# First batch's feed-forward first layer as three products of rounded parts, in a two-layer AdaLN kernel

## The chip, the cores and the metric

The kernel runs on one NeuronCore of one Trainium2 chip. The metric is the device time of one execution in microseconds (us). TensorE (PE in the profile, its weight loads PEld) does the matrix products, VectorE (DVE) and ScalarE (ACT) the elementwise work, GpSimd (POOL) some of it, SyncE (SP) issues the transfers.

## The reference, cut to what matters

The program is two transformer-like layers. The change lies in the soft mixture of experts of the first one. For each of B = 2 batches it takes S = 2048 rows x of width C = 256, normed and modulated, and e x t = 8 x 128 slots:

```
logits = jnp.einsum('bsd,etd->bset', xn, se)
dispatch = jax.nn.softmax(logits, axis=1)
slots = jnp.einsum('bsd,bset->betd', xn, dispatch)
h = jax.nn.gelu(slots @ w1, approximate=False)      # w1: 256 x 1024
processed = h @ w2                                  # w2: 1024 x 256
combine = jax.nn.softmax(logits.reshape(b, s, e * t), axis=-1)
out = jnp.einsum('bnd,bsn->bsd', processed.reshape(b, e * t, d), combine)
```

`slots @ w1` is the feed-forward's first layer; only that of batch 0 is touched. All data is float32.

## The kernel before, in words

There is no scheduler. Each engine has a program written out by hand, in order, and semaphores join them. The function `soft_mixture` does this stage, batch after batch (b = 0, 1), and within a batch in three parts.

First, eight turns, one for each expert (`et` = 0 to 7). In a turn TensorE makes the logits of the next expert (`logits`, four banks of 512 columns in `pL`), ScalarE copies them to `raw[et]` (`keep`), VectorE takes their maxima (`maxima`) and ScalarE the exponentials (`exps`, tile `work`). TensorE turns the exponentials of the current expert in four groups (`transposes`), ScalarE copies the first two turned groups and VectorE the last two (`copy_t`, tile shown as `mod`), and TensorE multiplies them with xn (`slots`). VectorE divides by the sum (`scale_slots`); TensorE turns the result, and VectorE copies it into `slotsT` (`d_sp`; experts 0 to 3 in `d_sp0`, 4 to 7 in `d_sp1`). VectorE also keeps a running maximum over experts in `top` (`tops`).

Second, the feed-forward: `hidden(b, a, j)` is slots times w1 for half a of the slots (512 columns) and piece j of 8 of the hidden width, into one of four banks of `pL`; ScalarE applies the gelu from there (`gelu`); `outputs(b, et)` is the second layer. Between them `top` is turned, reduced and spread (`turn_tops`, `row_tops`, `spread_tops`), VectorE subtracts it from the logits (`shift`) and scales the outputs (`processed`), and ScalarE takes the exponentials (`weights`). Third, `combine` multiplies these with the processed slots, 16 tiles of rows.

The logits are made by `exact_matmul`: each float32 operand is split into a rounded part (type FR, fp32r, made by ScalarE: `turned_high`) and what is left of it (made by VectorE: `turned_low`, xTl = xT - xTh), and three products replace one:

```
    nc.tensor.matmul(out, ah, bh, start=start, stop=False)
    nc.tensor.matmul(out, al, bh, start=False, stop=False)
    return nc.tensor.matmul(out, ah, bl, start=False, stop=stop)
```

`hidden` before uses one plain float32 product in place of these. Such a product shows as two records in the trace. The turned rows lie in `xTh` and `xTl`. Once the last logits of a batch are read (`l_ready`), SyncE loads `w1` and `w2` over `xTl` (`feed_forward`), and `xTh` lies unused until the next batch's rows are turned.

## Time and profile before

| | |
|---|---|
| median of 3 executions | 1737.71 us (1735.82 to 1738.24) |
| the profiled execution's own time | 1735.53 us |
| its span in the trace | 1733.8 us |
| mean granted TensorE clock | 0.985 |
| PE busy, DVE busy, ACT busy, POOL busy | 94%, 70%, 42%, 31% |
| soft mixture, batch 0: eight turns | about 389 to 511 us of the span |
| its feed-forward | about 511 to 573 us |
| its combine, with the next batch's rows turned | about 573 to 632 us |

Times in the views are microseconds from the span's start. An idle time in square brackets is that of the engine before the instruction, with what ended it.

### The profile page before, as it was taken

Reading aid. Unit: us, or ns where it says so; the run is one execution under the profiler, and the core shown is the slowest. Engines: PE = TensorE matmul, PEld = TensorE weight load, DVE = VectorE, ACT = ScalarE, POOL = GpSimd, SP = SyncE. Lnnn points to the kernel's source line nnn. Section 1 sums busy time; section 2 is a strip of 40 time slices with the busy share of each in tenths; the row PEclk is TensorE's granted clock in tenths of the full one; section 3 lists DMA queues with packets and bytes.
Section 4 is the critical chain, followed back from the end, with each engine's and each line's share of the span. In section 5 each row is a group of like instructions: output and inputs, shape, how many; then the busy total and the mean of one; then the engine's idle time right before and its main releaser. Section 6 shows DMA issues by size and latency. Waiting matters only on the chain. (4 is left out here: it accounts for less than half of the span.)

```text
span 1733.8 us, 25488 instructions
## 1 busy us (share of the span) xinstructions
PE 1637.8 (94%) x9248; PEld 1378.4 (80%) x9248; DVE 1208.5 (70%) x2665; ACT 732.7 (42%) x1443; POOL 541.5 (31%) x443
## 2 busy tenths in 40 slices
PE   6999989989999999999988999999989999999996
PEld 4688878888876888867876888888768788989895
DVE  5777677764544556656797899999967945666663
ACT  3333333434323434435436666666521324454442
POOL 2100020000000002332344666566400023777764
PEclk9999999999999999999999999999989999999998
DMA  6000000010010000031115222222241124666553
GB/s 225 4 1 1 1 1 1 1 43 7 0 49 0 1 13 13 19 107 55 33 50 203 65 76 76 78 82 83 62 153 55 49 64 142 154 146 162 136 123 37
DMA packets 80248, 111.55 MB, mean 64 GB/s; under 512 B 15982, under 2 KB 60154, under 8 KB 79868
## 3 DMA queue, kind: packets, MB, share of 16 engines
q1 hardware_dynamic: 66172, 91.43, 16.5%
q0 software_dynamic: 12288, 17.31, 5.6%
q8 instruction: 75, 1.23, 0.3%
q10 hardware_dynamic: 1664, 1.18, 0.2%
q14 instruction: 49, 0.40, 0.1%
HBM read 81.59 MB, written 27.68 MB: 63 GB/s over the span
## 5 line engine op out<-in xcount | busy, mean ns | idle before, releaser
L2994 POOL DMA_INDIRECT out<-k_eo,idx x64 | 117.2, 1832 | 75.5 <-DVE k_eo L3086 60.8
L1883 POOL DMA_INDIRECT k_xe<-rows_dram,idx x64 | 82.4, 1288 | 179.5 <-DVE idx L2927 141.2
L1716 PE MATMUL d_pO<-d_sp,d_raw 128*128 128x257 f32 x512 | 116.1, 384 | 1.9 <-DVE x L1197 1.7
L1716 PEld LDWEIGHTS d_pO<-d_sp,d_raw 128*128 128x128 f32 x512 | 96.9, 192 | 16.6 <-DVE x L1197 2.4
L537 ACT ACTIVATE b_p<-b_pS,b_nmax 128x2048 f32<-128x2048 f32 (+14 forms) x32 | 40.6, 1270 | 139.8 <-DVE b_nmax L678 139.8
L61 PE MATMUL b_pO<-b_vh,b_ph 128*128 128x256 f32 x302 | 87.9, 291 | 4.4 <-DVE b_pl L660 4.3
L62 PE MATMUL b_pO<-b_vh,b_pl 128*128 128x256 f32 x302 | 85.6, 283 | 0.0
L63 PE MATMUL b_pO<-b_vl,b_ph 128*128 128x256 f32 x302 | 85.6, 283 | 0.0
L333 POOL TENSOR_TENSOR x<-x,b_vrow 128x256 f32<-128x256 f32 x32 | 24.0, 780 | 186.4 <-DVE b_hs L606 186.3
L2076 ACT ACTIVATE g_dlm<-d_cumb,mod 128x128 f32<-128x128 f32 x256 | 78.5, 395 | 3.6 <-DMA d_cumb<-cum_dram 3.6
L3045 ACT ACTIVATE k_act_g<-k_pg 128x512 f32<-128x512 f32 x64 | 38.3, 598 | 88.6 <-PE k_pu L63 88.6
L3099 DVE TENSOR_TENSOR k_hid<-k_act_g,k_pu 128x512 f32<-128x512 f32 x64 | 44.0, 688 | 44.2 <-ACT k_act_g L3045 43.6
L61 PE MATMUL k_po<-k_wh,k_hh 128*128 128x256 f32 x256 | 72.4, 283 | 2.1 <-issue 2.1
L1482 ACT COPY d_raw<-pL 128x512 f32<-128x512 f32 x64 | 37.4, 588 | 86.5 <-PE pL L63 86.5
L63 PE MATMUL k_po<-k_wl,k_hh 128*128 128x256 f32 x256 | 72.5, 283 | 0.0
L62 PE MATMUL k_po<-k_wh,k_hl 128*128 128x256 f32 x256 | 72.4, 283 | 0.0
L669 DVE TENSOR_REDUCE b_part<-b_pS 128x1 f32<-128x512 f32 (+3 forms) x86 | 53.1, 624 | 27.2 <-PE b_pS L63 26.8
L61 PE MATMUL b_pS<-b_kh,b_qh 128*128 128x512 f32 (+3 forms) x172 | 69.3, 403 | 1.4 <-DVE b_vl L652 1.4
L61 PE MATMUL pL<-d_winh,g_uh 128*128 128x128 f32 (+1 forms) x186 | 68.4, 368 | 0.2 <-DVE d_cs L2305 0.2
L660 DVE TENSOR_TENSOR b_pl<-b_pT,b_ph 128x512 fp32r<-128x512 f32 (+3 forms) x86 | 50.4, 619 | 25.0 <-ACT b_ph L529 25.0
L63 PE MATMUL pL<-d_winl,g_uh 128*128 128x128 f32 (+1 forms) x186 | 66.8, 359 | 0.0
L62 PE MATMUL pL<-d_winh,g_ul 128*128 128x128 f32 (+1 forms) x186 | 66.5, 358 | 0.0
(555 smaller groups left out, 5270.3 us busy)
## 6 DMA issues: line engine op xcount, KB each, us to landing
d_cumb<-cum_dram SPq DMA_DIRECT2D x32, 512.0 KB, 4.2
k_wf<-in_WgT SPq DMA_DIRECT2D x16, 512.0 KB, 3.9
k_wf<-in_WuT SPq DMA_DIRECT2D x16, 512.0 KB, 4.9
k_wf<-in_WdT SPq DMA_DIRECT2D x16, 512.0 KB, 6.8
rows_dram<-h_hx SPq DMA_DIRECT2D x32, 136.0 KB, 3.8
x<-in_x SPq DMA_DIRECT2D x8, 512.0 KB, 10.5
d_w<-in_w SPq DMA_DIRECT2D x4, 1024.0 KB, 6.2
uT_dram<-d_ug SPq DMA_DIRECT2D x16, 256.0 KB, 2.4
```

Of the source, the lines that this page charges most:

```text
L61: nc.tensor.matmul(out, ah, bh, start=start, stop=False)
L62: nc.tensor.matmul(out, al, bh, start=False, stop=False)
L63: return nc.tensor.matmul(out, ah, bl, start=False, stop=stop)
L537: nc.scalar.activation(pr[:, n % 2, 0:w], pS[:, bank[n]:bank[n] + w], ACT.Exp, bias=nmax[:, n % 2:n % 2 + 1], scale=scale, accum_out=esum[ ...
L660: nc.vector.tensor_tensor(pl[:, r, 0:w], src[:, 0:w], ph[:, r, 0:w].bitcast(F32), ALU.subtract).then_inc(s["lo_done"], 1)
L669: nc.vector.reduce_max(part[:, n % 2, g:g + 1], pS[:, bank[n] + g * GW:bank[n] + g * GW + width(n, g)], axis=AX).then_inc(s["part_done"], 1)
L1716: last = nc.tensor.matmul(pO[:, t % 2, 0:PW], raw[e][:, t * P:(t + 1) * P], proc[e], start=e == 0, stop=e == E - 1)
L1883: nc.gpsimd.indirect_dma_start(out=m.xe[:, e % 2, t, :], out_offset=None, in_=m.rows, in_offset=bass.IndirectOffsetOnAxis(ap=column(m, e, ...
L2076: nc.scalar.activation(le[:, b, h, :], cumb[:, b, h, :], ACT.Relu, bias=cs[:, b, 3, h:h + 1], scale=-1.0).then_inc(s["dd_done"], 1)
L2994: nc.gpsimd.indirect_dma_start(out=out, out_offset=bass.IndirectOffsetOnAxis(ap=column(m, e, t), axis=0), in_=eo[:, e % 2, t, :], in_offse ...
L3045: nc.scalar.activation(act_g[:, f % 2], pg[:, f % 2], ACT.Gelu).then_inc(s["gelu_done"], 1)
L3099: nc.vector.tensor_tensor(hid[:, f % 2], act_g[:, f % 2], pu[:, f % 2], ALU.mult).then_inc(s["hid_done"], 1)
```

## The change: what it does

- `hidden` of batch 0 uses `exact_matmul` on rounded parts and remainders of w1 and of the slots: 3 fp32r products for each float32 product (96 in place of 32). Batch 1 is as before.
- ScalarE rounds w1 (`first_weights_high`, two instructions) and the first half of the slots (`slots_high_of(0)`) after its last copy of turn 7, and the second half (`slots_high_of(1)`) after the third gelu. They are put where `xTh` lay.
- VectorE makes the remainders in place, over w1 and over the slots: `first_weights_low(0)` and `(1)` behind each of its two copies in turn 7, `slots_low(0)` behind these, `slots_low(1)` between the two `row_tops`.
- In batch 0 `tops(et)` moves from the end of turn et to its start (from the middle of turn 7 for et = 7).
- The semaphores `xT_high` and `xT_low` count the new parts too (SPLIT = 4), and each piece of `hidden` waits for `xT_low`.

```diff
+        sp0_at = nc.sbuf_base - ES * PW * 4
...
+        w1l = placed("w1l", [P, CH, HID], xTl_at, FR)
+        slots_lows = [placed(f"slots_low{a}", [P, CH, 512], at, FR) for a, at in enumerate((sp0_at, area + 136 * KB))]
+        w1h = placed("w1h", [P, CH, HID], area + 44 * KB, FR)
+        slots_high = [placed(f"slots_high{a}", [P, CH, 512], area + (52 + 4 * a) * KB, FR) for a in range(SH)]
...
+            def first_weights_low(k):
+                dve.wait_ge(s["xT_high"], NG + k + 1)
+                nc.vector.tensor_tensor(w1l[:, k], w1[:, k], w1h[:, k].bitcast(F32), ALU.subtract).then_inc(s["xT_low"], 1)
+
+            def slots_low(a):
+                dve.wait_ge(s["xT_high"], NG + CH + a + 1)
+                nc.vector.tensor_tensor(slots_lows[a][:], slotsT[a], slots_high[a][:].bitcast(F32), ALU.subtract).then_inc(s["xT_low"], 1)
...
                 for et in range(E):
+                    if not b and et:
+                        tops(b, et)
                     if b and 2 <= et < E - 1:
                         step_sizes(0, et - 2)
...
                     for g in range(2, NG):
                         copy_t(b, ("exp", et, g))
-                    if et == E - 1:
+                        if not b and et == E - 1:
+                            first_weights_low(g - 2)
+                    if not b and et == E - 1:
+                        slots_low(0)
+                    if b and et == E - 1:
                         tops(b, et)
                     scale_slots(b, et)
...
-                    elif et:
+                    elif b and et:
                         tops(b, et)
...
                 row_tops(b, 0)
+                if not b:
+                    slots_low(1)
                 row_tops(b, 1)
...
+            def first_weights_high(k):
+                act.wait_ge(s["w_in"], 32)
+                act.wait_ge(s["l_ready"], bank(0, E - 1, NG - 1))
+                nc.scalar.copy(w1h[:, k], w1[:, k]).then_inc(s["xT_high"], 1)
+
+            def slots_high_of(a):
+                await_copy(act, at[0, "slots", (a + 1) * ES - 1, 0])
+                nc.scalar.copy(slots_high[a][:], slotsT[a]).then_inc(s["xT_high"], 1)
...
+                    elif not b:
+                        for k in range(CH):
+                            first_weights_high(k)
+                        slots_high_of(0)
...
                 for j in range(HT):
                     gelu(b, 0, j)
+                    if not b and j == 2:
+                        slots_high_of(1)
...
+                dst, of = pL[:, j % 4 * 512:(j % 4 + 1) * 512], slice(j * P, (j + 1) * P)
+                if not b:
+                    pe.wait_ge(s["xT_low"], NG + CH + a + 1)
                 for k in range(CH):
-                    last = nc.tensor.matmul(pL[:, j % 4 * 512:(j % 4 + 1) * 512], w1[:, k, j * P:(j + 1) * P],
-                                            slotsT[a][:, k, :], start=k == 0, stop=k == CH - 1)
+                    if b:
+                        last = nc.tensor.matmul(dst, w1[:, k, of], slotsT[a][:, k, :], start=k == 0, stop=k == CH - 1)
+                    else:
+                        last = exact_matmul(nc, dst, w1h[:, k, of], w1l[:, k, of], slots_high[a][:, k, :],
+                                            slots_lows[a][:, k, :], k == 0, k == CH - 1)
```

What stands in a row on an engine is shown at three places. The first is TensorE's, at the start of batch 0's feed-forward, behind the turning of `top`; before:

```order
L1697 MATMUL d_pT<-ident,d_top_4961 128x128 x7
L1677 MATMUL pL<-d_sp0,d_w1_4964 128x512 [waits d_w_in,d_raw_done]
L1677 MATMUL pL<-d_sp0,d_w1_4964 128x512 x7
L1704 MATMUL d_pT<-ident,d_rmax 128x128 [waits d_rmax_done]
L1704 MATMUL d_pT<-ident,d_rmax 128x128 x7
```

The same place in the changed kernel, its first pieces:

```order
L1740 MATMUL d_pT<-ident,d_top_4961 128x128 x7
L61 MATMUL pL<-d_slots_high0_4970,d_w1h_4969 128x512 [waits d_xT_low,d_w_in,d_raw_done]
L62 MATMUL pL<-d_slots_high0_4970,d_w1l_4966 128x512
L63 MATMUL pL<-d_slots_low0_4967,d_w1h_4969 128x512
L61 MATMUL pL<-d_slots_high0_4970,d_w1h_4969 128x512
L62 MATMUL pL<-d_slots_high0_4970,d_w1l_4966 128x512
L63 MATMUL pL<-d_slots_low0_4967,d_w1h_4969 128x512
L61 MATMUL pL<-d_slots_high0_4970,d_w1h_4969 128x512 [waits d_xT_low]
```

Each piece j (two products before) has become six, and the first of each waits for the remainders as well.

The second place is VectorE's turn 7 of batch 0, from the copy that ends turn 6 on; before:

```order
L1163 COPY d_sp1_4974<-d_pT 128x2x128 [waits d_t_ready]
L1154 TENSOR_TENSOR d_top_4961<-d_top_4961,d_raw6_4971 128x2048 [waits d_top_done,d_raw_done]
L1161 COPY mod<-d_pT 128x512 [waits d_t_ready] x2
L1154 TENSOR_TENSOR d_top_4961<-d_top_4961,d_raw7_4972 128x2048 [waits d_top_done,d_raw_done]
L1170 RECIPROCAL d_rsum<-d_esum 128x1 [waits d_exp_done]
L1175 TENSOR_SCALAR mod<-d_pO,d_rsum 128x256 [waits d_t_ready,d_sl_ready,d_rsum_done]
L1163 COPY d_sp1_4974<-d_pT 128x2x128 [waits d_t_ready] x2
L1180 TENSOR_REDUCE d_rmax<-d_pT 128x8 [waits d_mt_ready] x2
```

The same place in the changed kernel:

```order
L1177 COPY d_sp1_4980<-d_pT 128x2x128 [waits d_t_ready]
L1168 TENSOR_TENSOR d_top_4961<-d_top_4961,d_raw7_4978 128x2048 [waits d_top_done,d_raw_done]
L1175 COPY mod<-d_pT 128x512 [waits d_t_ready]
L1126 TENSOR_TENSOR d_w1l_4966<-d_w1_4964,d_w1h_4969 128x1024 [waits d_xT_high]
L1175 COPY mod<-d_pT 128x512 [waits d_t_ready]
L1126 TENSOR_TENSOR d_w1l_4966<-d_w1_4964,d_w1h_4969 128x1024 [waits d_xT_high]
L1130 TENSOR_TENSOR d_slots_low0_4967<-d_sp0,d_slots_high0_4970 128x1024 [waits d_xT_high]
L1184 RECIPROCAL d_rsum<-d_esum 128x1 [waits d_exp_done]
L1189 TENSOR_SCALAR mod<-d_pO,d_rsum 128x256 [waits d_t_ready,d_sl_ready,d_rsum_done]
L1177 COPY d_sp1_4980<-d_pT 128x2x128 [waits d_t_ready] x2
L1194 TENSOR_REDUCE d_rmax<-d_pT 128x8 [waits d_mt_ready]
L1130 TENSOR_TENSOR d_slots_low1_4968<-d_sp1_4980,d_slots_high1_4971 128x1024 [waits d_xT_high]
```

One maximum has left the place between the copies and the reciprocal (the one ahead of the copies is now that of expert 7), and three subtractions have come in, one of them between the two copies.

The third place is ScalarE's, from the last two copies of turn 7 on; before:

```order
L1487 COPY mod<-d_pT 128x512 [waits d_t_ready] x2
L1493 ACT_TABLE_LOAD
L1493 ACTIVATE d_work_4973<-pL 128x512 [waits d_h_ready] x5
L1497 COPY d_top_4961<-d_pT 128x1024 [waits d_mb_ready]
L1493 ACTIVATE d_work_4973<-pL 128x512 [waits d_h_ready] x3
```

The same place in the changed kernel:

```order
L1518 COPY mod<-d_pT 128x512 [waits d_t_ready] x2
L1496 CAST d_w1h_4969<-d_w1_4964 128x1024 [waits d_l_ready,d_w_in] x2
L1500 CAST d_slots_high0_4970<-d_sp0 128x1024 [waits d_t_copied_d]
L1524 ACT_TABLE_LOAD
L1524 ACTIVATE d_work_4979<-pL 128x512 [waits d_h_ready] x3
L1500 CAST d_slots_high1_4971<-d_sp1_4980 128x1024 [waits d_t_copied_d]
L1524 ACTIVATE d_work_4979<-pL 128x512 [waits d_h_ready] x2
```

Three roundings stand ahead of the table load, and one among the gelus.

## Rows read from the trace of the kernel before

**Rows 1.** The page's busy times of TensorE and of its weight loads.

```profile
PE 1637.8 (94%) x9248; PEld 1378.4 (80%) x9248; DVE 1208.5 (70%) x2665; ACT 732.7 (42%) x1443; POOL 541.5 (31%) x443
```

**Rows 2.** TensorE's waits from 559.6 us to the end, the longest two.

```profile
PE pL L2424 <- ACT mod L2055: 4.8, 1, 4.8
PE i_pg L61 <- PEq L50: 3.0, 1, 3.0
```

**Rows 3.** TensorE's groups by form, 384 to 900 us: busy us, mean ns.

```profile
L1677 PE MATMUL pL<-d_sp,d_w 128*128 128x512 f32 x128 | 56.1, 593 | 0.0
L61 PE MATMUL pL<-d_xTh,o_seh 128*128 128x512 f32 x128 | 51.4, 402 | 0.0
```

**Rows 4.** TensorE by stretches: two of logits, then two of `hidden`.

```profile
439.29:444.87 5.58, 5.58 (x24) 1.00 0.00 0
632.53:643.55 11.02, 11.02 (x51) 1.00 0.00 0
511.50:518.37 6.87, 6.87 (x16) 1.00 0.00 0
544.98:558.90 13.92, 13.89 (x32) 1.00 0.00 0
```

**Rows 5.** Timeline of turn 7: start us, duration us.

```profile
500.97 0.59 ACT L1487 COPY mod<-d_pT 128x512 f32<-128x512 f32 x1 [0.64 <-PE d_pT L1657]
501.57 1.28 ACT L1493 ACT_TABLE_LOAD   x1
503.13 0.69 DVE L1161 COPY mod<-d_pT 128x512 f32<-128x512 f32 x1 [0.72 <-PE d_pT L1657]
505.10 3.62 PE L1667 MATMUL d_pO<-o_keys,mod 128*128 128x256 f32 x16
505.30 0.69 DVE L1161 COPY mod<-d_pT 128x512 f32<-128x512 f32 x1 [1.47 <-PE d_pT L1657]
505.91 2.28 DVE L1154 TENSOR_TENSOR d_top<-d_top,d_raw 128x2048 f32<-128x2048 f32 x1
508.11 0.15 DVE L1170 RECIPROCAL d_rsum<-d_esum 128x1 f32<-128x1 f32 x1
509.07 0.48 DVE L1175 TENSOR_SCALAR mod<-d_pO,d_rsum 128x256 f32<-128x256 f32 x1 [0.81 <-PE d_pT L1661]
513.42 0.60 ACT L1493 ACTIVATE d_work<-pL 128x512 f32<-128x512 f32 x1 [10.57 <-PE pL L1677]
```

**Rows 6.** Groups by form of roundings and subtractions elsewhere in this stage.

```profile
L1539 ACT CAST d_wogh<-d_wog 128x1024 fp32r<-128x1024 f32 x2 | 2.0, 1035 | 0.0
L1277 DVE TENSOR_TENSOR d_wogl<-d_wog,d_wogh 128x1024 fp32r<-128x1024 f32 x2 | 2.4, 1224 | 0.0
```

**Rows 7.** All engines by stretches while w1 and w2 arrive; DMA share, GB/s last.

```profile
489.90:495.00 5.10, 4.81 (x29) 4.06 (x28) 1.69 (x4) 3.62 (x5) 0.00 (x0) 1.00 0.77 261
495.00:497.50 2.50, 2.50 (x15) 2.27 (x14) 0.76 (x2) 0.00 (x0) 0.00 (x0) 1.00 0.90 307
497.50:499.00 1.50, 1.50 (x10) 1.27 (x9) 0.00 (x0) 0.00 (x0) 0.00 (x0) 1.00 0.00 0
```

**Rows 8.** Timeline of VectorE in turn 1, and one row of turn 2.

```profile
409.82 0.48 DVE L1175 TENSOR_SCALAR mod<-d_pO,d_rsum 128x256 f32<-128x256 f32 x1 [2.77 <-PE d_pO L1667]
411.74 0.69 DVE L1142 TENSOR_REDUCE d_part<-d_raw 128x1 f32<-128x512 f32 x1 [1.44 <-ACT d_raw L1482]
...
427.67 1.27 DVE L1142 TENSOR_REDUCE d_part<-d_raw 128x1 f32<-128x512 f32 x2
```

**Rows 9.** Timeline from the last shifts to the first combine.

```profile
546.39 8.89 DVE L1185 TENSOR_TENSOR d_raw<-d_raw,d_top 128x2048 f32<-128x2048 f32 x4
559.56 14.08 PE L1685 MATMUL d_pO<-d_w,d_work 128*128 128x256 f32 x64 [0.69 <-ACT d_work L1493]
560.82 14.51 ACT L1501 ACTIVATE d_raw<-d_raw 128x2048 f32<-128x2048 f32 x8
573.48 14.07 PE L1716 MATMUL d_pO<-d_sp,d_raw 128*128 128x257 f32 x64
```

**Rows 10.** All engines by stretches at the start of the last stage; granted clock behind POOL.

```profile
1435.00:1437.00 2.00, 0.00 (x0) 0.00 (x0) 1.22 (x1) 0.00 (x0) 0.00 (x0) 1.00 0.00 0
1437.00:1439.00 2.00, 1.78 (x5) 1.48 (x6) 0.00 (x0) 0.00 (x0) 0.96 (x2) 0.68 1.08 269
1439.00:1441.00 2.00, 2.00 (x6) 1.55 (x5) 0.00 (x0) 0.00 (x0) 1.70 (x2) 0.50 0.88 278
```

More of the change, by code:

```diff
@@ L905, in soft_mixture @@
         NH = NTB // 2
+        SPLIT = CH + SH
         upper_half = pL[:, HALF:T].rearrange("p (k n) -> p k n", k=CH)
@@ L1132, in turned_low @@
                 cols = slice(g * GW, (g + 1) * GW)
-                dve.wait_ge(s["xT_high"], n)
+                dve.wait_ge(s["xT_high"], n + (SPLIT if b else 0))
                 if b:
@@ L1630, in turn @@
                     if g >= 2:
-                        pe.wait_ge(s["xT_low"], NG + g - 1)
+                        pe.wait_ge(s["xT_low"], NG + SPLIT + g - 1)
                 elif g == NG - 1:
@@ L1756, in _ @@
                 for g in range(NG):
-                    pe.wait_ge(s["xT_low"], b * NG + (NG if b and g >= 2 else g + 1))
+                    pe.wait_ge(s["xT_low"], b * (NG + SPLIT) + (NG if b and g >= 2 else g + 1))
                     logits_of(0, g).then_inc(s["l_ready"], 1)
```

## The prediction

> **What bounds the kernel now.** I read the page first. TensorE is busy 94% of the span and its weight loads 80%; VectorE is next with 70% [rows 1]. So a microsecond taken from TensorE's own queue is worth a microsecond, unless a wait behind it grows. I then looked at the stretch around the change, 384 to 632 us, by groups, by stretches and in order of time. In both stretches of `hidden` TensorE never stops: 6.87 us busy of 6.87, and 13.89 of 13.92, at a granted clock of 1.00 (the level of 2.4 GHz) [rows 4]. The reader should see in the timeline that ScalarE sat idle for 10.57 us before the first gelu and that VectorE had gaps too [rows 5]: nothing but TensorE's rate sets the length of `hidden`. Last I asked what TensorE waits for behind the stage: the longest waits are 4.8 and 3.0 us, on ScalarE and on its own sequencer [rows 2]. I found no transfer issued before 511 us, other than w1, w2 and the spill of x, that something later waits for, so no late event of fixed time stands ready to swallow a gain.
>
> **The products removed.** Batch 0 has 2 x 8 x 2 = 32 plain products, 64 records. Their durations overlap (593 ns each [rows 3]), so the price is the distance between them: 16 records in 6.87 us, 0.4294 us a record [rows 4]. The first half is two such runs (4 pieces, the spreading of `top`, 4 pieces), 2 x 6.87 = 13.74 us. The second half is 32 records in one run, 13.74 us of the 13.92 without the drain. Together 27.48 us.
>
> **The products added.** 96 fp32r products of the same form, 128 x 128 weights and 512 columns. The trace has them in the logits (402 ns each by duration [rows 3]), in two lengths that fit: a run of 24 in 5.58 us, which includes the slower start behind other work, and a run of 48 in 11.02 us [rows 4]. Waits for a free bank are in these too, as in the new `hidden`. The first half is two runs of 24, 11.16 us; the second one run of 48, 11.02 us; together 22.18 us. **The gain is 27.48 - 22.18 = 5.30 us.**
>
> Bounds of this term. The second 24 of the run of 48 take 11.02 - 5.58 = 5.44 us, 0.2267 us each. If all 96 ran so, they would take 21.76 us and the gain would be 5.7. If each of the 16 pieces, because of its new wait on `xT_low`, paid the whole excess of a fresh start (5.58 - 5.44 = 0.14 us), it would be 2.2 us more: a gain of 3.5. I take 5.3, since the logits have a wait for each bank and show no such excess.
>
> A record of a plain product takes 0.4294 us, so two of them, 0.859 us, stand against three fp32r products at 0.2267 or more, 0.68 us. The Trainium skill ("FP8 and Floating Point Precision", TensorE Precision Notes) says that true float32 takes four passes through the array, and "TensorE: Matmul & The Clock Gate" (Back-to-back issue gap) gives 518 cycles for 512 columns, 216 ns at 2.4 GHz. By that the old term would be 128 x 0.216 = 27.6 us, which the trace bears out, and the new one 96 x 0.216 = 20.7 us, an estimate that gives a gain of 6.9 us; the rows of the logits show each fp32r product 5% to 8% slower than that, and they decide the sum.
>
> **ScalarE's four roundings.** A rounding of 128 x 1024 takes 1.035 us [rows 6]. The first three start when the last copy of turn 7 ends, at 501.57, and end by 504.7; the table load of 1.28 us then ends at 506.0. The first gelu comes at 513.42 [rows 5], so they cost nothing, with 7.4 us to spare. The fourth stands behind the third gelu. A piece will be ready every 11.02 / 8 = 1.38 us, and gelu plus rounding take 0.60 + 1.04 = 1.64 us: the fourth gelu is 0.3 us late once. TensorE needs its bank only four pieces later (5.5 us). Nothing.
>
> They wait for w1 and w2. These are issued once the last logits are read, at about 489.9 us. 261 GB/s over 5.1 us and 307 GB/s over 2.5 us are 2.1 MB, which is both tensors, and after 497.5 us the DMA engines are idle [rows 7]. ScalarE gets there at 501.57, 4.1 us later. Nothing, while that cover holds.
>
> **VectorE's four subtractions.** One takes 1.224 us [rows 6]. The first goes behind the copy at 503.13, which ends at 503.82; its rounding ended at 502.6; so it ends at 505.05, and the next copy starts at 505.30. That copy's follower starts at 505.91, as `tops` did [rows 5]. Two subtractions then stand where the maximum of 2.28 us stood: 505.91 + 2 x 1.224 = 508.36, plus 0.15 for the reciprocal, 508.5. The scaling waits for TensorE until 509.07, so 0.5 us of cover is left. If it were gone, the scaling, the last turned slots, the turning of `top` and all of `hidden` would be late by the same amount. The remainder that TensorE's first piece waits for is ready at 508.4; the piece starts at 511.50: 3.1 us to spare. The fourth subtraction stands between the two `row_tops`; the second of these waits for TensorE's second turning of `top`, which comes only behind all eight pieces, over 10 us later. Nothing.
>
> **The moved maxima.** In turns 2 to 7 the same place has the same work, with the index one higher. Only turn 1 gains one: 2.28 us behind the scaling of 409.82, so from 410.3 to 412.6. The first maximum of a bank started at 411.74 [rows 8] and will be 0.8 us late; the next banks come six products or 1.36 us apart and need 0.69, so VectorE has caught up at the third. Turn 2 already runs so: two reductions back to back in 1.27 us right behind `tops` [rows 8]. Nothing; the bound from the other side is the 0.8 us, if it did not catch up before the exponentials.
>
> **What follows.** The shifts end at 555.28 before [rows 9] and start 2.6 us earlier with the first half's gain. The gelus end 5.3 us earlier, so the exponentials start at 555.5 in place of 560.82; the last of the eight needs its shift about 12.7 us later. The outputs (14.08 us) and the combine hang on the last gelu as well and move with it [rows 9]. The whole 5.3 us goes through.
>
> **Sum.** The profiled execution took 1735.53 us (1733.8 us of span and 1.7 around it): 1730.2. It was 2.2 us under the median of 1737.71; from the median, 1732.4 us. I predict the latter. A measurement of this kernel can tell about 0.2% from no change, 3.5 us.
>
> **Where the clock comes in.** Nothing in the stage itself should change it: it is 1.00 there under both kinds of product [rows 4]. But at 1437 us, behind a stretch in which TensorE did nothing, the granted clock is 0.68 and 0.50 (1.2 GHz) for two stretches of 2 us [rows 10]; that costs (0.32 + 0.50) x 2 = 1.6 us. The change moves this place by 5.3 us, and the fall may be longer, shorter or missing: 1.6 us either way.
>
> **The rivals.**
> - *Three products at the pace of passes.* If an fp32r product costs half of a plain record, 0.2147 us, the 96 take 20.6 us and the gain is 6.9: 1730.8 us. The logits of this very form speak against it. The two pages of the Trainium skill named above would give this too. Chance 0.04.
> - *A partial gain.* The new wait of each piece, or VectorE's 0.5 us of cover in turn 7 overrun by up to 1 us, take 2 to 3.5 us together: 1734.4 to 1736. For it: the cover is thin, and VectorE's first subtraction depends on ScalarE. Against: each piece of that chain has its own row. Chance 0.10.
> - *The gain does not reach the end.* A wait behind the stage grows by what was gained: 1737.7 us. It would need something with a time of its own, and the list of waits names none. Chance 0.04.
> - *Slower.* The mechanism is w1 and w2 coming late: ScalarE's rounding waits, VectorE stands at its first subtraction with the last copy of turn 7 and the scaling queued behind it, and TensorE waits for these. The chain takes up 4.1 us (ScalarE), 1.2 (between rounding and copy), 0.2 and 0.5 (VectorE) = 6.0 us. The data may land up to 503.5 us free of cost; beyond that each us costs one. To end slower by 3.5 us it must eat 8.8, so land at 512.3, 22 us after the issue where the bytes now take under 8. Nothing else is on the DMA engines then. Landing at 515 us would give 1737.7 - 5.3 + 11.5 = 1743.9 us. Chance 0.03.
>
> **How the numbers follow.** The forecast, a gain of 4 to 6 us, has the remaining 0.79. Faster by over 0.2% (under 1734.2 us): 0.79 less 0.03 for a median that lands high, plus 0.04, plus 0.02 of the partial case: 0.82. Within 0.2%: 0.14. Slower: 0.04 with the noise. The range takes the gain of 3.5 to 6.9 us, the clock's 1.6 us and the spread of the three runs before (1.9 under the median, 0.5 over): from 1729.2 to 1736.5 us, which leaves out about 0.15.
>
> **What the profile after would show.** Right: groups of `hidden` with x96 in three lines at about 392 to 402 ns, runs of 24, 24 and 48 in 5.6, 5.6 and 11.0 us; the casts at 501.6 us without a wait; the scaling in turn 7 still waiting for TensorE at 509.1; the first piece at 511.5; the first combine at 568.2; the last logits of turn 2 unchanged. Wrong: a product's distance over 0.24 us; a wait of TensorE on a subtraction; a scaling that starts late in turn 7; a wait of ScalarE for DMA ahead of the casts; a clock below 1.00 between 511 and 554 us; or a wait after 632 us that was not there.

## The result and the profile after

The changed kernel took **1725.72 us** (median of 4 runs, 1724.98 to 1727.6), the kernel before 1736.76 us beside it (4 runs, 1734.83 to 1738.24): a ratio of 0.9953, 95% interval 0.9933 to 0.9972. The gain is real, and it is larger than the 5.3 us that I forecast. Later measurements repeated it: 0.9959 (0.9944 to 0.9975), 0.9951 (0.9938 to 0.9965), 0.9953 (0.9941 to 0.9966). Over all of them the mean is 1734.6 us for the kernel before (123 runs, twice its standard error is 0.5) and 1727.0 us for the changed one (25 runs, 0.8): **7.5 us, plus or minus 0.9**. Taken sitting by sitting, the means differ by 10.6 us (four and four runs), 7.3 and 7.7 us (9 and 12 runs of the changed kernel). The profiled execution took 1727.6 us, its span 1725.9.

The page's busy times, to be set against [rows 1]: TensorE is busy 7.2 us less, VectorE and ScalarE 4.4 and 3.6 us more.

```profile
PE 1630.6 (94%) x9280; PEld 1383.8 (80%) x9280; DVE 1212.9 (70%) x2669; ACT 736.3 (43%) x1447; POOL 543.0 (31%) x443
```

TensorE's groups by form between 384 and 900 us (busy us, mean ns). `hidden` of batch 0 now stands in three lines of 32. Each product lasts as long as those of the logits, in the line on top.

```profile
L61 PE MATMUL pL<-d_xTh,o_seh 128*128 128x512 f32 x128 | 51.4, 402 | 0.0
L61 PE MATMUL pL<-d_slots_high,d_w1h 128*128 128x512 f32 x32 | 12.8, 401 | 0.0
L63 PE MATMUL pL<-d_slots_low,d_w1h 128*128 128x512 f32 x32 | 12.5, 391 | 0.0
L62 PE MATMUL pL<-d_slots_high,d_w1l 128*128 128x512 f32 x32 | 12.5, 391 | 0.0
```

The same three stretches of `hidden` as in [rows 4]: us, TensorE busy, its weight loads, VectorE, ScalarE, GpSimd, granted clock, DMA. Two runs took 5.61 and 5.63 us (6.87 before), the second half 11.16 (13.92 before), and TensorE never stops in them.

```profile
511.76:517.37 5.61, 5.61 (x27) 4.60 (x26) 1.23 (x1) 2.38 (x4) 0.00 (x0) 1.00 0.00 0
519.07:524.70 5.63, 5.63 (x27) 4.41 (x25) 0.00 (x0) 2.60 (x4) 0.00 (x0) 1.00 0.00 0
542.44:553.60 11.16, 11.16 (x50) 8.99 (x48) 10.42 (x13) 4.19 (x7) 0.00 (x0) 1.00 0.00 0
```

Turn 7 by the timeline (start us, duration us), against [rows 5]. The casts start without a wait, the subtractions fill the place of the maximum, and the scaling at 509.42 still waits for TensorE.

```profile
501.31 0.59 ACT L1518 COPY mod<-d_pT 128x512 f32<-128x512 f32 x1 [0.64 <-PE d_pT L1694]
501.79 2.00 ACT L1496 CAST d_w1h<-d_w 128x1024 fp32r<-128x1024 f32 x2
503.69 1.05 ACT L1500 CAST d_slots_high<-d_sp 128x1024 fp32r<-128x1024 f32 x1
504.08 1.22 DVE L1126 TENSOR_TENSOR d_w1l<-d_w,d_w1h 128x1024 fp32r<-128x1024 f32 x1
506.25 1.22 DVE L1126 TENSOR_TENSOR d_w1l<-d_w,d_w1h 128x1024 fp32r<-128x1024 f32 x1
507.38 1.22 DVE L1130 TENSOR_TENSOR d_slots_low<-d_sp,d_slots_high 128x1024 fp32r<-128x1024 f32 x1
509.42 0.48 DVE L1189 TENSOR_SCALAR mod<-d_pO,d_rsum 128x256 f32<-128x256 f32 x1 [0.74 <-PE d_pT L1698]
511.76 0.48 PE L61 MATMUL pL<-d_slots_high,d_w1h 128*128 128x512 f32 x1
```

The first combine, 573.48 us in [rows 9], comes at 568.30, though batch 0's soft mixture began 0.35 us later (385.39 against 385.04 us). TensorE's longest waits behind the stage are those of [rows 2], with none on the change's tiles. The row of `d_pO` counts one wait more than in that profile of the kernel before, 1.5 us at 886.41 us in batch 1's combine. It is not the change's: the kernel before has it too in its profile `b0_again`, and not in the three in which the clock fell at 874 us.

```profile
568.30 1.47 PE L1759 MATMUL d_pO<-d_sp,d_raw 128*128 128x257 f32 x6
```

```profile
PE pL L2467 <- ACT mod L2098: 4.8, 1, 4.8
PE d_pO L1759 <- DVE x L1211: 3.3, 2, 1.7
PE i_pg L61 <- PEq L50: 3.0, 1, 3.0
```

So the stage does what was forecast, and the rest of the gain is elsewhere. To find it I set the same TensorE instructions of all profiles beside each other. The table gives the time between the starts of six of them, in us: the start of the span to the soft mixture of batch 0 (385.04 in the kernel before); to turn 7's last sums (505.10); to the first combine (573.48), which holds the changed work; to a product of the state space stage (1258.98); over the border to the next stage (1279.95); to a product of the last stage (1699.94). The last column is a distance inside "later": from the product `pL<-g_bcT` at 946.03 us to the first product `g_pyT<-d_wogh,g_yh` behind it, 947.42. Each number is a difference of two start times in that profile's timeline. The names below the changed kernel's four profiles are those of the experiments.

```
                     start  to505  stage  later   border  rest    946-947
before              385.04 120.06  68.38  685.50  20.97  419.99   1.39
b0_again            383.93 119.95  68.37  686.81  20.96  419.96   1.39
b1_more             383.35 119.95  68.38  687.52  20.70  420.06   1.40
b2_more             383.84 119.94  68.38  687.07  20.43  419.94   1.39
changed             385.39 120.05  62.86  684.39  19.28  420.02   0.38
a0_again            384.48 119.95  62.87  684.48  19.28  419.97   0.48
a1_more             385.81 120.04  62.88  684.05  19.30  420.01   0.41
a2_more             384.65 119.94  62.88  684.05  22.55  420.01   0.20
products_only       385.77 120.06  62.78  685.34  19.03  418.40   1.39
prep_only           384.63 120.05  68.39  684.72  19.00  418.36   0.48
prep_again          386.23 120.03  68.39  685.02  20.46  419.90   0.49
half_products       385.43 120.06  65.57  685.67  19.03  418.43   1.39
six_more            381.67 119.98  73.54  686.21  19.26  419.92   0.93
six_fewer           384.36 119.98  68.38  682.64  19.24  419.89   1.40
changed_six_fewer   385.56 119.95  62.87  684.15  22.54  420.02   0.44
four_tiny           381.39 120.04  68.38  684.62  20.65  419.96   0.20
one_tiny            381.34 119.94  68.38  685.24  19.31  420.08   0.53
changed_four_tiny   384.90 119.96  62.83  686.31  19.27  419.97   0.56
```

The stage column is as steady as clockwork: 68.38 against 62.87, **5.50 us**, in four profiles of each. Between the means of the four profiles the other columns give: start -1.0, later +2.5 (of it 1.0 in the last column), border +0.7, rest 0. Nothing of the change lies in the start, so its 1.0 us the wrong way is chance. Of the other 1.5 us of "later", most stands in falls of the clock that single profiles have and others of the same kernel do not: about 1.6 us each at 762 us in `b1_more` and `b2_more`, about 1.4 at 946 us in `b0_again`.

### The profile page after: what moved, and what is told of

It is laid out like the page before. It is cut to its first block and busy times, and to the rows that moved or that the text cites. A ratio compares the mean times of both kernels' runs of the same rounds, so it can differ in the third digit from the quotient of the medians.

```text
span 1725.9 us, 25574 instructions
## 1 busy us (share of the span) xinstructions
PE 1630.6 (94%) x9280; PEld 1383.8 (80%) x9280; DVE 1212.9 (70%) x2669; ACT 736.3 (43%) x1447; POOL 543.0 (31%) x443
## 3 DMA queue, kind: packets, MB, share of 16 engines
q8 instruction: 75, 1.23, 0.3%
## 5 line engine op out<-in xcount | busy, mean ns | idle before, releaser
L537 ACT ACTIVATE b_p<-b_pS,b_nmax 128x2048 f32<-128x2048 f32 (+14 forms) x32 | 40.6, 1270 | 142.0 <-DVE b_nmax L678 142.0
L2728 ACT ACTIVATE i_act_g<-i_pg 128x512 f32<-128x512 f32 x30 | 17.9, 598 | 114.2 <-PE i_pu L63 114.2
```

The costliest lines, as they stand in the source:

```text
L537: nc.scalar.activation(pr[:, n % 2, 0:w], pS[:, bank[n]:bank[n] + w], ACT.Exp, bias=nmax[:, n % 2:n % 2 + 1], scale=scale, accum_out=esum[ ...
```

## The experiments

The theories. **A**: the products pay 5.3 us, and what the kernel gained beyond them is where the clock happened to fall. **B**: what comes earlier makes later falls of the clock shorter, in each run. **C**: the work that was moved or added pays by itself. **D** came later, below.

**1. The two kernels again.** No edit.

> The changed kernel once more, for its time over more runs. In the profile the first combine starts 5.2 us earlier than before, which is the sum's term; a further 2.7 us of the 7.9 us of span come after 1250 us of the span, where TensorE's clock stands at 0.50 for a shorter time. Theory A (the products alone pay, the rest is chance in where the clock falls): the ratio over more runs is about 0.997, 5.3 us, and the stretch at 0.50 near 1260 us is long in some profiles and short in others. Theory B (the change moves the later stages so that the clock falls for a shorter time in every run): the ratio stays at 0.994 to 0.995, 9 to 10 us, and the stretch near 1260 us is as short as in the first profile, about 4 us.

> The kernel before, unchanged, as a control: ratio 1.000 within 0.001 by both theories. Theory B expects the same long stretch at 0.50 near 1264 to 1278 us in its profile as in the first one (some 12 us); theory A has no reason for it and allows any length.

Measured: the changed kernel 1729.15 us (9 runs), the kernel before 1735.99 (12 runs of this copy) and 1735.52 (30 runs beside them). The gain stays above 5.3 us. My expectation put the 2.7 us beyond the stage all behind 1250 us; the table shows 1.1 of them between 573 and 1259 us in the first pair of profiles. The kernel before moves by 11 us among its own runs (1729.5 to 1741.1), which is more than the whole change, so a mean needs many runs.

**2. The preparation without the products, and the products without the preparation.**

The edits, cut to what matters (`...` marks what is left out):

```
prep_only, against the changed kernel
-                    if b:
...
-                        last = exact_matmul(nc, dst, w1h[:, k, of], w1l[:, k, of], slots_high[a][:, k, :],
-                                            slots_lows[a][:, k, :], k == 0, k == CH - 1)
+                wk, sk = (w1[:, k, of], slotsT[a][:, k, :]) if b else (w1h[:, k, of].bitcast(F32), slots_high[a][:, k, :].bitcast(F32))
+                last = nc.tensor.matmul(dst, wk, sk, start=k == 0, stop=k == CH - 1)
products_only, against the kernel before
...
+                    if b:
+                        last = nc.tensor.matmul(dst, w1[:, k, of], slotsT[a][:, k, :], start=k == 0, stop=k == CH - 1)
+                    else:
+                        last = exact_matmul(nc, dst, xTh[:, k, of], xTh[:, k, of], xTh[:, k, 0:512],
+                                            xTh[:, k, 0:512], k == 0, k == CH - 1)
```

> All of the change but its products: the roundings, the subtractions, the moved maxima and the waits stay, and the first batch's first layer is 64 plain records again, on the rounded parts alone (the remainders are left out of the product). Theories A and B: the stage is as long as before, the first piece starts at 511.5 us within 0.3 and the first combine at 573.5; ratio 1.000 within 0.001. Theory C (part of the gain comes from the moved work, a shorter turn or an earlier gelu): ratio 0.997 to 0.998.

> Only the products of the change: three fp32r products for each plain one in batch 0's first layer, but of the turned rows xTh in place of the weights and slots, so there is nothing to round, no moved maxima and no new wait. Theory A: 5.3 us, ratio 0.997. Theory B: the same ratio as the changed kernel in this job, since the later stages are moved by the same 5.3 us. Theory C: 2 to 4 us less gain than the changed kernel.

Measured: `prep_only` 1730.78 us (12 runs), a ratio of 0.9972 (0.9960 to 0.9984); `products_only` 1727.39 us (10 runs), 0.9958 (0.9941 to 0.9975). `products_only` multiplies rows that lie ready, so it leaves out the roundings, the subtractions, the moved maxima and the added waits. `prep_only` looked like theory C: 4 us for work that only adds. But its stage takes 68.39 us, as before. What its profile gained lies in other places: a missing fall of the clock in the last stage (418.36 against 420.0), the border (19.00 against 21.0), and a microsecond near 947 us. The products alone give 5.60 us in the stage.

**3. Other amounts of TensorE's time, and at another place.** Half of the new products; six plain products more in the stage; six plain products fewer in batch 1's `hidden` (three in each half of the slots), in both kernels.

```
half_products: as products_only, with
...
+                    if not b and not a:
six_more, against the kernel before
+                    if not b and not k and j < 3:
+                        nc.tensor.matmul(pL[:, j % 4 * 512:(j % 4 + 1) * 512], w1[:, k, j * P:(j + 1) * P],
+                                         slotsT[a][:, k, :], start=True, stop=True)
six_fewer, against the kernel before, and changed_six_fewer, against the changed one
+                    if b and j < 3 and k:
+                        continue
...
```

> The kernel before, in which the first batch's hidden products of the first four experts alone (16 of 32 plain ones) are three rounded products each, of rounded inputs that lie ready, in place of the weights and slots: the output is not the reference's. No preparation, no added wait. TensorE takes 2.6 us less there. Theory A (the rest beyond 5.3 us in the changed kernel is chance in where the clock falls): 2.6 us faster than the kernel before, 1732.9 us against 1735.5, the mean granted clock over the runs that of the kernel before (0.9855), and the profile has either length of fall at the border near 1262 to 1278 us. Theory B (work that comes earlier makes that fall short, in each run): 4.5 to 5.5 us faster, 1730 to 1731 us, the clock over the runs 0.0012 higher, the fall at the border 1.7 us in the profile.

> The kernel before with 6 more plain hidden products in the first batch (their results are overwritten by the products that follow): 6 times 0.859, 5.15 us more of TensorE's time in the stage that the change shortens. Theory A: 5.2 us slower than the kernel before, 1740.7 us against 1735.5, clock over the runs the same. Theory B in its plain form (what comes later falls longer): 7 us or more slower, clock over the runs lower than 0.9855; in its form of a place that is passed by (any shift shortens the fall): 3 us slower, clock higher.

> The kernel before, in which 6 plain hidden products of the second batch are left out (the second half of the sum for 6 of its 32 groups, so the output is not the reference's): 5.15 us less of TensorE's time, taken near 860 us instead of near 530. Theory A: 5.2 us faster, 1730.3 us against 1735.5, or less if the 1.5 us by which a shift before 878 us can be absorbed at 891 us counts; the clock over the runs as before. Theory B: 7.5 us faster, 1728 us, the clock over the runs 0.0012 higher, the fall at the border short in the profile, since what lies before the border is shifted as in the changed kernel. Theory C (the moved work of the change pays): 5.2 us and no more.

> The changed kernel with the same 6 products of the second batch left out (output not the reference's). Theory A: 10.5 us faster than the kernel before, 1725.0 us against 1735.5. Theory B: 12.5 to 13 us faster, 1722.5 to 1723 us; and if the length of the fall goes up and down with the shift rather than being long at none and short at any, the fall is long again in this profile or in that of the half products.

Measured, beside 24 runs of the kernel before with 1733.11 us: half 1731.34 us (12 runs, 0.9993, 0.9982 to 1.0003), six more 1739.86 (7 runs, 1.0028, 1.0015 to 1.0042), six fewer 1732.01 (12 runs, 0.9992, 0.9981 to 1.0003), changed with six fewer 1727.22 (6 runs, 0.9956, 0.9940 to 0.9971). The stage is linear in TensorE's work: 2.81 us for the half, -5.16 for six more, 5.50 for all. The whole kernel's time resolves six more, and not the half. Theory B in its strong form falls: six products *more* leave a short border (19.26), and the changed kernel with six fewer has a long one (22.54).

Six fewer in batch 1 gave 2.6 us (682.64 in "later" against 685.50, of which 0.3 lies behind 830 us) and not 5.15. The first half of the slots gave all of it, the second (at 798 us in the kernel before, not near 860 as I expected) nothing. TensorE's timeline of `six_fewer` shows why: the first product of the fifth piece waits for a gelu.

```profile
795.09 4.46 PE L1679 MATMUL pL<-d_sp,d_w 128*128 128x512 f32 x10
801.99 1.55 PE L1679 MATMUL pL<-d_sp,d_w 128*128 128x512 f32 x3 [2.44 <-ACT d_work L1493]
```

That product needs the bank of the first piece, which the first gelu of this half reads. Ahead of this gelu ScalarE has the next stage's weights and two table loads:

```profile
796.21 2.20 ACT L1531 CAST d_winh<-d_win 128x1152 fp32r<-128x1152 f32 x2
...
798.52 1.28 ACT L1534 ACT_TABLE_LOAD   x1
...
800.04 1.28 ACT L1493 ACT_TABLE_LOAD   x1
801.34 2.06 ACT L1493 ACTIVATE d_work<-pL 128x512 f32<-128x512 f32 x4
```

In `changed_six_fewer` the same wait of 2.44 us was followed at once by 3.4 us at a granted clock of 0.50, and only 0.9 us of the six products was left behind it. Its time, 1727.22 us, is that of the changed kernel: neither theory's number (1725.0, or 1722.5 to 1723) came.

**4. More runs and profiles.** No edit.

> The changed kernel once more, beside new runs of the kernel before. Theory A, as it stands after eight kernels (the change gives 5.3 us of TensorE's time; what was measured beyond it is where the clock happened to fall in those executions): 5.3 us faster than the kernel before of the same job, plus or minus 1.5, and a fall of the clock of either length at the border near 1255 to 1270 us in the profile. Theory B (the changed kernel falls less, as a property of its timing): 7 to 7.5 us faster again, the mean granted clock over the runs 0.001 higher than that of the kernel before, the fall at the border short in the profile.

> The changed kernel again, for a second profile and as many runs more; expected is what is expected of the other one. The two together make some 20 runs, whose mean is known to about 1 us: theory A 5.3 us below the kernel before, theory B 7 to 7.5 us.

> The kernel before once more, for a third profile. Theory A: the fall near 1262 to 1278 us is short in some profiles of the kernel before; with one more look it may be either. Theory B: long again, 6.8 us.

> The kernel with all of the preparation, the moved maxima and the added waits, but plain products, once more: it measured 4 us faster than the kernel before in an earlier job, where its own trace shows no step that took less time, only other falls of the clock. Theory A: no faster than the kernel before now, within 1.5 us. Theory C (the moved work pays by itself): 4 us faster again.

Measured: changed 1726.16 and 1726.39 us (6 runs each), before 1733.97 (23 runs beside them) and 1734.38 (12 runs), preparation alone 1732.74 (11 runs, 0.9991, 0.9982 to 1.0000). So the gain is 7.5 to 8 us again. Theory A as I had it falls too, since the products give 5.5 us of it and chance alone would not repeat the rest. And preparation alone gave 1.2 us this time, not 4. Here the last column of the table came up. The distance 946-947 is 1.39 or 1.40 us in six of the seven profiles so far of kernels without the preparation (0.93 in the seventh, `six_more`) and 0.20 to 0.49 in all seven with it. The timeline of the kernel before shows what lies in it:

```profile
942.46 0.15 DVE L2238 TENSOR_SCALAR h_rs<-h_mv 128x1 f32<-128x1 f32 x1
942.69 0.55 POOL L2023 TENSOR_TENSOR h_rs<-h_rs,neghalf 128x1 f32<-128x1 f32 x1 [1.61 <-DVE h_rs L2238]
942.92 1.23 DVE L2198 TENSOR_TENSOR g_dlm<-g_dlm,mod 128x1024 f32<-128x1024 f32 x1 [0.31 <-issue]
943.21 1.84 POOL L2010 TENSOR_TENSOR g_wide<-g_wide,mod 128x512 f32<-128x512 f32 x1
944.06 1.27 DVE L2182 TENSOR_TENSOR g_ul<-uT,g_uh 128x256 fp32r<-128x256 f32 x1
946.70 0.67 DVE L2209 TENSOR_TENSOR g_yl<-g_pyT,g_yh 128x512 fp32r<-128x512 f32 x1
947.42 0.38 PE L61 MATMUL g_pyT<-d_wogh,g_yh 128*128 128x256 f32 x1 [0.95 <-DVE g_yl L2209]
```

The same rows in the changed kernel:

```profile
937.25 0.15 DVE L2281 TENSOR_SCALAR h_rs<-h_mv 128x1 f32<-128x1 f32 x1
937.36 1.23 DVE L2241 TENSOR_TENSOR g_dlm<-g_dlm,mod 128x1024 f32<-128x1024 f32 x1
937.49 1.50 POOL L2066 TENSOR_TENSOR h_rs<-h_rs,neghalf 128x1 f32<-128x1 f32 x1 [1.66 <-DVE h_rs L2281]
938.50 0.42 DVE L2225 TENSOR_TENSOR g_ul<-uT,g_uh 128x256 fp32r<-128x256 f32 x1
938.96 1.04 POOL L2053 TENSOR_TENSOR g_wide<-g_wide,mod 128x512 f32<-128x512 f32 x1
940.47 0.67 DVE L2252 TENSOR_TENSOR g_yl<-g_pyT,g_yh 128x512 fp32r<-128x512 f32 x1
941.20 0.39 PE L61 MATMUL g_pyT<-d_wogh,g_yh 128*128 128x256 f32 x1
```

Before, VectorE stands for 0.31 us in front of the multiplication of `g_dlm`, though nothing that the trace knows holds it ("issue"). GpSimd's tiny power gets in first and takes 0.55 us; its next operation (1.84 us in place of 1.04) then runs against VectorE's rounding remainder, which takes 1.27 us in place of 0.42. In the changed kernel VectorE is first, the tiny power stretches to 1.50 us where nobody waits for it, and `g_yl`, on which TensorE waits, is a microsecond earlier. That microsecond lasts: `products_only`, level with the changed kernel up to 936 us within 0.3, is 0.9 us behind it from 945 us to the border. What the two groups of kernels do not share ahead of this place is ScalarE's four roundings, the moved maxima and VectorE's four subtractions. Hence **theory D**: it is only the number of VectorE instructions ahead.

**5. Fills that nobody reads.** In the kernel before, in batch 0's soft mixture (one, or four); and four in the changed kernel; and the kernel before once more.

```
+        tiny = placed("tiny", [P, 4], area + 60 * KB)
...
                 row_tops(b, 0)
+                if not b:
+                    for k in range(4):
+                        nc.vector.memset(tiny[:, k:k + 1], 0.0)
                 row_tops(b, 1)
```

> The kernel before with four fills of one number a partition on VectorE in the first batch's soft mixture, where the change puts a subtraction; nothing else of the change, and the fills are read by nobody. Theory D (VectorE has a hole of 0.31 us in front of a multiplication by the decay near 943 us in each of seven kernels without the change's four subtractions and in none of seven with them; in the hole GpSimd gets ahead, and the subtraction behind takes 1.27 us in place of 0.42, which makes TensorE 1.0 us late at 947 us; what decides is how many VectorE instructions stand ahead): the hole is gone and the first output product after it (947.4 us in the kernel before) comes 1.0 us earlier relative to what precedes it. Over the runs at equal clock about 1 us faster. Rival (it is the time at which the stage is reached, or the casts on ScalarE): the hole stays, as in the kernel before.

> The same with one fill in place of four: theory D says the hole of 0.31 us depends on the number of VectorE instructions ahead; with one it may stay or go, which tells how near the edge the kernel before stands. The time is that of the kernel before within its spread (1729 to 1741 us). A look at the clock at the border near 1262 us as well: theory A has it short in some profiles, theory B long in each kernel whose stages lie as in the kernel before.

> The changed kernel with four such fills in addition, eight VectorE instructions more than the kernel before. Theory D: the hole comes back only if eight stand as none does; otherwise the multiplication and the subtraction behind it take 1.2 and 0.42 us as in the changed kernel. 1724 to 1731 us. The fall of the clock at the border: short in three of four profiles of the changed kernel so far.

> The kernel before, a fourth profile. The hole of 0.31 us on VectorE near 943 us is there again (theory D). Fall of the clock at the border 1262 to 1278 us: theory A short in some profile, theory B 5.1 to 6.8 us again.

Measured: with four fills the hole is gone, with one it is 0.05 us, so that VectorE is first by 0.04 us (939.57 against 939.61), and the distance 946-947 is 0.20 and 0.53 us. The kernel before in its fourth profile has the hole and 1.39 us again. The fills bring no rounding and no moved maximum, so these are not needed for it. The time at which the place is reached does not decide either: the multiplication starts between 937.89 and 945.44 us in the eight profiles with the hole, and between 936.20 and 944.33 us in the ten without. VectorE and GpSimd in `four_tiny`:

```profile
938.97 0.15 DVE L2242 TENSOR_SCALAR h_rs<-h_mv 128x1 f32<-128x1 f32 x1
939.08 1.23 DVE L2202 TENSOR_TENSOR g_dlm<-g_dlm,mod 128x1024 f32<-128x1024 f32 x1
939.21 1.50 POOL L2027 TENSOR_TENSOR h_rs<-h_rs,neghalf 128x1 f32<-128x1 f32 x1 [1.65 <-DVE h_rs L2242]
940.22 0.42 DVE L2186 TENSOR_TENSOR g_ul<-uT,g_uh 128x256 fp32r<-128x256 f32 x1
942.18 0.67 DVE L2213 TENSOR_TENSOR g_yl<-g_pyT,g_yh 128x512 fp32r<-128x512 f32 x1
```

The hole has not vanished for good, it has moved. In all eight profiles with four VectorE instructions more than the kernel before, one of 0.27 us stands at another instruction, where the ten others have none; in the changed kernel:

```profile
1309.45 0.69 DVE L2982 TENSOR_TENSOR i_hid<-i_act_g,i_pu 128x512 f32<-128x512 f32 x1 [0.27 <-issue]
```

Counted over everything that the trace has of VectorE, semaphore instructions included, the holes stand at entries 1728 and 2496 in the kernel before (942.92 and 1234.32 us) and 2752 in the changed one: 768 and 256 apart. All 24 holes of 0.27 to 0.31 us in the eighteen profiles stand at one of these three entries. The kernel before is also 0.27 us late at its own entry 2752 (1318.31 us), another instruction there, which the trace puts down to the instruction ahead of it. So the place goes by multiples of 256 entries, as far as these rows tell. With one fill, entry 1728 is the semaphore instruction ahead of the multiplication, and 0.1 us of delay shows there.

In time, `four_tiny` took 1733.16 us (12 runs) against 1733.48 (17 runs), 0.9996 (0.9984 to 1.0008): a microsecond cannot be told that way. The single executions took 1729.82 us (`one_tiny`), 1728.77 (`changed_four_tiny`) and 1735.03 (`b2_more`).

**The clock taken out.** Each of 228 runs lists its span and its mean granted clock. A straight line with one slope for all kernels gives 1.0 us of span for each 0.001 of clock, with 1.3 us of scatter left. Compared at equal clock, the gain over the kernel before (119 runs) is 6.7 us for the changed kernel (25), 5.7 for the products alone, 0.7 for the preparation alone (23), 1.2 for four fills, 3.2 for the half, -4.3 for six more, each plus or minus 0.6 to 1.0. The stage and the 946-947 distance make 5.5 + 1.0 = 6.5 for the changed kernel. That leaves 7.5 - 6.5 = **1.0 us, plus or minus 0.9**, for the clock, which is hardly told from nothing.

**The border.** Stretches of 2 us; the granted clock is the third number from the right. The kernel before loses 2 x (0.09 + 6 x 0.50 + 0.32) = 6.8 us of clock between 1262 and 1278 us:

```profile
1262.00:1264.00 2.00, 1.92 (x10) 1.64 (x11) 1.05 (x3) 0.60 (x4) 0.00 (x0) 0.91 0.40 135
1270.00:1272.00 2.00, 0.00 (x0) 0.00 (x0) 1.32 (x3) 0.00 (x0) 0.00 (x0) 0.50 0.00 0
1274.00:1276.00 2.00, 2.00 (x7) 1.62 (x6) 0.16 (x1) 0.00 (x0) 0.00 (x0) 0.50 1.03 289
1276.00:1278.00 2.00, 2.00 (x7) 1.58 (x7) 1.14 (x5) 0.00 (x0) 0.00 (x0) 0.68 0.85 298
```

The changed kernel loses 1.7 us at the same place of the program:

```profile
1264.00:1266.00 2.00, 0.74 (x3) 0.63 (x4) 0.72 (x4) 0.77 (x1) 0.50 (x3) 0.92 0.00 0
1266.00:1268.00 2.00, 2.00 (x8) 1.62 (x6) 0.23 (x2) 0.28 (x1) 0.00 (x0) 0.50 0.73 230
1268.00:1270.00 2.00, 2.00 (x8) 1.63 (x8) 1.30 (x6) 0.00 (x0) 0.00 (x0) 0.73 1.04 403
```

But `a2_more`, the same program, has it at 0.50 from 1256 to 1270 us, 8.5 us lost in all:

```profile
1254.00:1256.00 2.00, 1.54 (x7) 1.31 (x6) 0.36 (x3) 0.72 (x3) 0.00 (x0) 0.68 0.57 190
1264.00:1266.00 2.00, 0.00 (x0) 0.00 (x0) 1.18 (x2) 0.00 (x0) 0.00 (x0) 0.50 0.00 0
1270.00:1272.00 2.00, 2.00 (x6) 1.52 (x5) 0.99 (x5) 0.00 (x0) 0.00 (x0) 0.56 0.97 362
```

And the kernel before in `b2_more` loses 2 x (0.27 + 0.50 + 0.50 + 0.43) = 3.4 us:

```profile
1268.00:1270.00 2.00, 0.33 (x1) 0.14 (x1) 1.11 (x3) 0.93 (x3) 0.00 (x0) 1.00 0.23 79
1270.00:1272.00 2.00, 0.20 (x1) 0.23 (x2) 0.65 (x4) 0.23 (x1) 0.17 (x2) 0.73 0.00 0
1276.00:1278.00 2.00, 2.00 (x6) 1.57 (x6) 0.33 (x4) 0.28 (x1) 0.00 (x0) 0.57 1.00 357
```

The border column follows the loss: 19.0 to 19.3 us with 1.7 lost, 20.4 to 20.7 with 3.4, 20.7 with 5.1 (`b1_more`), 21.0 with 6.8, 22.5 with 8.5. So one program has long and short falls, and each of these profiles can be nothing more than its draw. Still, 3.4 us or more were lost in four of four profiles of the kernel before and in four of the fourteen others; whether the kernel before is prone to it stays open.

## Why the prediction was right, and where it was wrong

- **What bounds the kernel**: right. TensorE's work in the stage turns into time one for one, in both directions (2.81, 5.50 and -5.16 us for 16, 32 and six products).
- **The term of the sum**: right. Forecast 5.30 us, measured 5.50 from 505 us to the first combine. The runs took 5.61, 5.63 and 11.16 us with their last product's end; forecast were 5.58, 5.58 and 11.02 for 24, 24 and 48. The bound of a fresh start for each piece (2.2 us more, a gain of 3.5) did not come: the new waits on `xT_low` cost nothing. The rival of three products at the pace of passes asked for 6.9 us in the stage, and the stage gave 5.50: the nearest rows decided rightly against it, though the time of the whole kernel would have seemed to speak for it.
- **ScalarE's roundings, w1 and w2, the moved maxima**: right, at nothing. The first cast starts at 501.79 us behind the copy, not behind a transfer; the stretch to 505 us is 119.94 to 120.06 us in all eighteen profiles, so `tops` one place earlier costs nothing there.
- **VectorE's four subtractions**: right in the stage (the scaling at 509.42 waits for TensorE, 0.74 us), **wrong as "nothing"** for the kernel. They put every later instruction four places on in VectorE's program, the hole of 0.31 us at 943 us falls elsewhere, and TensorE gets 1.0 us there. `four_tiny` and `one_tiny` show it with no work worth naming. I priced the added instructions by their own time and cover only.
- **Where the clock comes in**: **this step failed**, and with it the range. I looked for falls at one place, 1437 us, and priced them at 1.6 us either way. That place did not change: "rest" is 419.9 to 420.1 us in fifteen profiles and 418.4 in three, which have no fall there. The falls that differ are near 762, 905 to 950 and 1262 to 1278 us, and one border alone spans 19.0 to 22.5 us, 3.5 us where I allowed 1.6. Mean to mean, the clock gave the changed kernel 1.0 us (plus or minus 0.9); in the four and four runs of the result chance gave more: their means, 1726.0 and 1736.65, lie 1.0 under and 2.1 over those of all runs.
- **Sum**: **this step failed too.** I subtracted from a median of three runs, 1737.71 us, which lies 3.2 us above the mean of 123; the same chance in the clock is in it. Of the 6.7 us between my 1732.4 and the measured 1725.72 us, 3.2 are this start, 2.2 are the gain that I missed (7.5 against 5.3), and 1.3 are four fortunate runs of the changed kernel, whose mean of 25 is 1727.0. By the steps as they are now known: 1734.6 - 5.5 - 1.0 = 1728.1 us, and 1.0 us for the clock. So the stage was understood, and the time of the whole kernel was not.
- **The range** took the clock at 1.6 us and the spread of three runs at 1.9; the kernel before alone spreads over 11 us. Its lower end does not follow from its own parts either: 1737.71 - 6.9 - 1.6 - 1.9 = 1727.3 us, not 1729.2. The measured median lies under both.

## What to carry to other kernels

When a kernel is bound by TensorE, price products by the distance between records in a full run of the same form; it held to 0.2 us in 5.5. Judge a gain of a few microseconds by the distance between two fixed instructions in several profiles, where one microsecond shows in each, and not by medians of three runs. Adding an instruction to an engine can shift who is first between VectorE and GpSimd hundreds of microseconds later: look there before a surplus is put down to the change's own work. And the same edit in batch 1 must not be priced by TensorE alone: with 5.15 us less work there only 2.6 us came back, because ScalarE's casts and table loads stand ahead of the second half's first gelu.

## What the runs showed of the hardware that was not expected

- A hole of 0.31 us on VectorE with nothing to wait for, at the same instruction in each of eight profiles of kernels with one length of VectorE program, and in none of ten with one, four or eight instructions more. A second one stands at 1234.32 us in the profile of the kernel before and costs nothing, and the one of 0.27 us at 1309.45 us in the changed kernel costs nothing either. They stand at multiples of 256 entries of VectorE from each other. What the engine does at these entries no run here shows.
- VectorE and GpSimd slow each other: the same subtraction of 128 x 256 took 0.42 us alone and 1.27 us beside GpSimd, a GpSimd power of 128 numbers 0.55 us when first and 1.50 us when second, a GpSimd multiplication 1.04 and 1.84 us. Being first by 0.13 us (0.04 in `one_tiny`) decided a whole microsecond. The Trainium skill ("SBUF — State Buffer", SBUF: two separate sides) says that the two share a pair of ports as an exclusive lock, which whoever starts first keeps for the whole instruction while the other waits, a VectorE operation with two inputs in SBUF against a GpSimd one that reads SBUF. The trace agrees for the power behind the multiplication (1.50 us) and, roughly, for the subtraction behind GpSimd's (1.27 us). It does not show it for the multiplication of the kernel before, which starts at 942.92 us, 0.32 us ahead of the power's recorded end, and takes 1.23 us as ever. Part of the 0.31 us could by that rule be GpSimd's power holding the ports; but the multiplication starts 0.11 us behind the start of the instruction ahead of it in the changed kernel (937.25 to 937.36), and by that it should have started at 942.57 in the kernel before, ahead of the power at 942.69. By these rows the lateness begins on VectorE.
- Some of TensorE's lost clock costs nothing: with a fall at 874 to 878 us (three of four profiles of the kernel before) TensorE is 1.7 us later at 889 us and level again at 892, where it otherwise waits 1.5 us for VectorE (886.41 us in the changed kernel).
